# The last batch of a cross-attention and FFN kernel: row sums ahead of the last tile's products, and VectorE normalising straight out of the accumulator

## What is computed

```python
# x (8, 56, 128), ctx (8, 1500, 128), mask (8, 56); all float32
xn = layernorm(x)
q, k, v = heads(xn @ Wq), heads(ctx @ Wk), heads(ctx @ Wv)      # 16 heads of 64
dots = q @ k.T * 64 ** -0.5 - (1 - mask)[:, None, :, None] * 1e6
x = x + merge(softmax(dots) @ v) @ Wout + bout
z = layernorm(x)
x = x + gelu(z @ w1[e] + b1[e]) @ w2[e] + b2[e]                 # e = the batch
```

## Time and profile before

| | |
|---|---|
| three runs | 405.58, 407.91, 409.17 us; median 407.91 us |
| the profiled execution's own time | 405.75 us |
| its span, first to last instruction | 403.9 us |
| PE busy | 390.0 us (97%), 1721 MATMUL records |
| DVE busy | 302.8 us (75%) |
| ACT busy | 206.0 us (51%) |
| mean granted TensorE clock | 1.000 of full speed |
| chain that ended last, by engine | PE 90%, DVE 5%, ACT 2% |

### The profile page before, as it was taken

The page is one execution under the profiler, slowest core; times in us unless marked ns, Lnnn a source line. Parts: engine busy times, 40 slices in busy tenths (PEclk is TensorE's granted clock), DMA queues, the critical chain, the costliest instruction groups (busy, mean ns, idle before and its releaser), DMA issues.

```text
span 403.9 us, 5555 instructions
## 1 busy us (share of the span) xinstructions
PE 390.0 (97%) x1721; PEld 281.2 (70%) x1721; DVE 302.8 (75%) x490; ACT 206.0 (51%) x274; POOL 57.6 (14%) x47
## 2 busy tenths in 40 slices
PE   7998999999999999999999999999999999999995
PEld 6665666767675877767776877667766777676684
DVE  4889678877887689877887689787887686365443
ACT  3546354565457444665455454565357444746431
POOL 0603400600060000600060001500150000000000
PEclk9999999999999999999999999999999999999999
DMA  7660020040005000042004000160011001100000
GB/s 252 210 199 21 2 76 1 12 142 0 2 4 148 2 2 2 25 155 81 0 18 135 0 0 0 43 193 26 0 35 42 0 0 53 57 2 0 3 2 3
DMA packets 20661, 19.62 MB, mean 49 GB/s; under 512 B 904, under 2 KB 17576, under 8 KB 20648
## 3 DMA queue, kind: packets, MB, share of 16 engines
q1 hardware_dynamic: 20648, 19.45, 15.7%
HBM read 19.21 MB, written 0.23 MB: 48 GB/s over the span
## 4 chain that ended last, share of the span: by engine, by line
PE 90%; DVE 5%; ACT 2%; issue 1%; DMA 1%; SPq 0%; ACTq 0%; DVEq 0%
PE ps_a L426 35%; PE ps_s L398 28%; PE ps_x L434 10%; PE ps_x L453 4%; PE ps_x L441 3%; PE ps_a L373 2%; PE ps_x L473 2%; PE ps_x L482 2%; PE ps_s L412 2%; DMA ex<-in_wk_t 1%; DVE log_sum L793 1%; DVE ctxt_hi L782 1%; ACT inv_sum L635 1%; PE ps_s L528 1%; PE ps_x L412 1%
## 5 line engine op out<-in xcount | busy, mean ns | idle before, releaser
L426 PE MATMUL ps_a<-ex,ctx_sb 125*128 125x448 f32 x384 | 172.1, 541 | 0.0
L605 ACT ACTIVATE ex<-ps_s 125x896 f32<-125x896 f32 x96 | 88.0, 917 | 117.4 <-PE ps_s L398 91.3
L765 DVE TENSOR_REDUCE chunk_max<-ps_x 128x1 f32<-128x500 f32 x168 | 111.3, 674 | 32.6 <-PE ps_x L434 29.5
L434 PE MATMUL ps_x<-ctxt_hi,qk_hi 128*128 128x500 f32 x168 | 88.5, 530 | 6.3 <-DVE log_sum L793 3.6
L426 PEld LDWEIGHTS ps_a<-ex,ctx_sb 125*128 125x128 f32 x384 | 71.4, 189 | 27.5 <-issue 21.6
L762 DVE TENSOR_TENSOR ex_sum<-ex_sum,ex 125x896 f32<-125x896 f32 x80 | 86.6, 1083 | 4.6 <-ACT ex L605 4.6
L398 PE MATMUL ps_s<-qk_hi,ctxt_hi 128*125 128x448 f32 x192 | 87.2, 535 | 0.0
L612 ACT COPY ps_s<-shift_row 125x896 f32<-125x896 f32 x80 | 72.9, 911 | 9.9 <-DVE shift_row L882 7.8
L398 PEld LDWEIGHTS ps_s<-qk_hi,ctxt_hi 128*125 128x125 f32 x192 | 35.8, 187 | 35.5 <-issue 35.1
L398 PE MATMUL ps_s<-qk_hi,ctxt_lo 128*125 128x448 f32 x192 | 57.3, 379 | 0.0
L1008 POOL TENSOR_TENSOR qk_lo<-qk,qk_hi 128x448 fp32r<-128x448 f32 x16 | 23.7, 1483 | 218.9 <-DVE qk_hi L786 218.1
(11 more groups left out here) (79 smaller groups left out, 263.3 us busy)
## 6 DMA issues: line engine op xcount, KB each, us to landing
ctxt_raw<-in_ctx_t SPq DMA_DIRECT2D x8, 750.0 KB, 7.4
ctx_sb<-in_ctx SPq DMA_DIRECT2D x8, 750.0 KB
w_sb<-in_w SPq DMA_DIRECT2D x4, 512.0 KB, 3.8
w_sb<-in_w SPq DMA_DIRECT2D x8, 256.0 KB, 4.4
ex<-in_wq_t SPq DMA_DIRECT2D x2, 256.0 KB, 3.9
ex<-in_wk_t SPq DMA_DIRECT2D x2, 256.0 KB, 4.8
att_n<-in_wv_t SPq DMA_DIRECT2D x1, 512.0 KB, 5.9
att_n<-in_w_out SPq DMA_DIRECT2D x1, 512.0 KB, 7.1
```

The lines of the kernel that those rows point to most:

```text
L426: mm = nc.tensor.matmul(ps_a[:, c, 0:CH], ctx_sb[0:MT, u, t, :], ex[0:MT, t % RING, c * CH:(c + 1) * CH], start=(t == 0), stop=(t == TM - 1))
L434: nc.tensor.matmul(bank[:, 0:MC], qk_hi[:, u, t * P:(t + 1) * P], ctxt_hi[:, u, k * MC:(k + 1) * MC], start=True, stop=True).then_inc(job_ ...
L605: nc.scalar.activation(half(ex[0:MT, slot, :]), src, ACT.Exp, scale=SCALE).then_inc(ex_ready, 1)
L765: nc.vector.tensor_reduce(chunk_max[:, k, t:t + 1], filled()[:, 0:MC], AX.X, ALU.max).then_inc(job_free, 1)
```

## The change

Three things, all behind the last batch's tiles. On TensorE the row sums (`sum_jobs`) go from behind the products of tile 11 to between those of tile 10 and tile 11, and `keep_clock(14)` ahead of `y_job` becomes `keep_clock(4)`. On ScalarE the copy `att_out` goes away. On VectorE a new `normalise_last` reads `ps_a` where `normalise_att` read `att`; it waits for the products of tile 11 itself (`pv_done`).

```diff
             iteration(last, prepare=False, pair=Pair(None, ROUNDS, half=0))
-            for t in range(TM - 2, TM):
-                probs_ctx(last, t)
+            probs_ctx(last, TM - 2)
             sum_jobs(last)
+            probs_ctx(last, TM - 1)
             pair = Pair(None, ROUNDS, half=1)
-            keep_clock(14)
+            keep_clock(4)
             y_job(pair)
...
             iteration(last, prepare=False, pair=Pair(None, ROUNDS, half=0))
-            att_out(last)
             inverse_sums(last)
...
+            def normalise_last(b, c):
+
+                dve.wait_ge(pv_done, b.at(TM, TM))
+                nc.vector.tensor_tensor(att_n[:, c * HP:(c + 1) * HP, TOK * b.parity:TOK * b.parity + N],
+                                        ps_a[:, c, 0:CH].rearrange("p (h n) -> p h n", n=N),
+                                        inv_sum[:, c * CH:(c + 1) * CH].rearrange("p (h n) -> p h n", n=N),
+                                        ALU.mult).then_inc(att_n_ready, 1)
...
                 drain_sum(last, c)
                 refine_inverse(c * HP, (c + 1) * HP)
-                normalise_att(last, c * HP, (c + 1) * HP)
+                normalise_last(last, c)
```

## The result

| | before | after |
|---|---|---|
| median of 13 runs | 406.21 us (405.34 to 409.17) | 404.16 us (403.56 to 406.46) |
| ratio | | 0.9946, 95% interval 0.9923 to 0.9968 |
| profiled execution: span | 403.9 us | 403.2 us |

The changed kernel is 0.54% faster; 0.47% (1.91 us) was forecast. The last additions of the two profiles differ by only 0.7 us, because this execution came 1.12 us later to the place where the change begins: the seventh batch's `out_job` starts at 379.06 before and at 380.18 after. Most of that difference is there by 38 us, in a part of the program that the change doesn't touch: the same exp of ScalarE (L605) starts at 37.22 before and at 38.31 after.

A forecast was written before the change was run, and what follows sets the result against it. The end was taken to be set by TensorE's fillers, with sums, logarithm, exp, drain, refine and normalise behind them. Gain 1.56 + 0.37 - 0.02 = 1.91 us gave 403.84 or 406.00, so 405.0 us in the middle, range 403.3 to 407.4.

The forecast's parts named there:

- Fillers on the chain, `y_job` held by 0.37 us: Ahead of y_job on TensorE: it could begin at 388.29 but fillers hold it until 388.66, 0.37 us.
- Sums 1.50 us earlier without a wait: TensorE's row sums, moved ahead of tile 11's four records, start 1.50 us earlier; last add_tile leaves 1.14 us of slack.
- The copy worth 0.06 us: ScalarE ahead of the logarithm: the 0.91 us copy lies beside the sums, so removing it gains only 0.06 us.
- The other half of that step: With sums ahead of tile 11, a copy must wait for tile 11 and would hold up a ready logarithm; edits belong together.
- VectorE out of the accumulator at no price: Normalising from PSUM costs the same as from SBUF, by rows of 620 and 625 ns; dearer normalisation had chance 0.12.
- The additional 65 ns for each: Estimate from the skill page: each of the two PSUM normalisations 65 ns longer, the gain some 0.1 us smaller; not adopted.
- The slack ahead of its wait: VectorE's first normalisation, newly waiting for tile 11's products, may start from 385.64, 0.32 us in time.
- The second half comes just in time: Within y_job: ninth head reached at 388.56, its input usable at 388.58, so a wait of 0.02 us.
- The gap ahead of `y_job`: With eight filler records, TensorE idles about 0.24 us before y_job, waiting for VectorE, in place of none.
- The clock: Granted clock stays 1.00 through y_job; rival: it falls behind eight fillers, 1.7 to 6.7 us slower, chance 0.05.
- My price for a fall through `y_job`: If the granted clock fell to 1.2 GHz in the gap, y_job would take 3.65 us more.
- The sum from the median of three runs: Whole kernel: median of three earlier runs less the 1.91 us gain, 406.00 us; upper of two sums around 405.0.

The follow-up runs named there:

- The copy kept: Kernel before with the sums ahead of tile 11 and 4 fillers, ScalarE's copy staying ahead of the logarithm; median 409.50 us, ratio to before 1.0064.
- the two kernels at 9.24 us: Kernel before with only keep_clock(14) cut to 4, and changed kernel with sums back behind tile 11; last addition ends at 22.71 and 22.70 us.
- the repeat: Changed kernel, unaltered, timed again beside a version with tile 11's halves apart; 12 runs, median 404.20 us, ratio to before 0.9968.
- the 3.3 us gap: TensorE idle ahead of y_job in the kernel before with early sums, 4 fillers and the copy kept; y_job took 5.35 us, ratio to before 1.0064.
- the 3.0 us gap: TensorE idle ahead of the transpose in the changed kernel without its three keep_clock calls; last addition at 22.89 us, ratio to before 1.0006.

## Why the prediction was right, point by point

**Fillers on the chain, `y_job` held by 0.37 us.** Right: 0.36 measured with the fillers alone.

**Sums 1.50 us earlier without a wait.** Right: the sum records start at 3.38 us from the anchor, where they were at 4.88. The moved matmuls are worth exactly their own length, 9.24 to 7.73 between late and early sums.

**The copy worth 0.06 us.** Wrong in size: it is 0. I had taken the 0.04 us from the end of the products to the copy, and put the same between the first sum and a logarithm without the copy. The logarithm starts 1.01 us after the first sum record with the copy (before: 383.94 to 384.95) and without it (after: 383.56 to 384.57). From the end of the second sum record, as the profile counts it, that is 0.09 us and not 0.04 (after: 383.94 + 0.54 = 384.48 to 384.57). In the kernel before, the copy would have let it go at the same moment: where the logarithm waited for the copy alone ("The copy kept"), it started 0.80 us after the copy's start, and 384.14 + 0.80 is 384.94. So it moved by 1.50 us and not by 1.56. The other half of that step, that the copy may not stay once the sums are early, was right and matters more: 10.73 in place of 7.73.

**VectorE out of the accumulator at no price.** Right: 624 ns, against 624 to 626 from SBUF. The additional 65 ns for each that I had worked out from the Trainium skill ("Perfetto Trace Analysis", Optimizing Scalar/DVE Operations) doesn't show, neither here nor between the two kernels at 9.24 us. The slack ahead of its wait was there too, 0.27 us where I had 0.32: with the chain 0.75 us earlier, it becomes an idle of 0.48.

**The second half comes just in time.** Right: `y_job` takes 3.72 us where it took 3.71, so the ninth head waits for next to nothing.

**The gap ahead of `y_job`.** I said 0.24 and it is 0.29: `y_job` came 0.06 later than forecast, as the logarithm did.

**The clock.** Right for this change, granted 1.00 through `y_job`. The step behind it, that a longer gap is needed for a fall, was shown from both sides: no fall behind 1.18, 1.80 and 1.82 us, a fall behind 3.01 and, in eight of nine executions as far as their mean clock tells, behind 3.30. Nothing between 1.82 and 3.01 us was run. My price for a fall through `y_job` was too high, 3.65 us where 1.63 was measured, because the clock fell only within `y_job` and came back within it.

**The absolute time.** 405.0 forecast, 404.16 measured. The sum from the median of three runs (406.00) was high since two of those three were over 407.5; with the median of 13, 406.21 less 1.91 is 404.30. The 405.0 was the middle between two sums and rested on no mechanism. That the medians differ by 2.05 us, so near the forecast, owes something to luck: the tails differ by 1.86, and the repeat gave 1.73. The spread that I could not explain lies in part in the opening, in its waits and its clock.

## What to carry to other kernels

When fillers stand on the chain of waits, the path behind them is the true bound: find the wait that they cover, shorten the path, and cut the fillers with it. Here the shorter path without fewer fillers gave nothing, and fewer fillers without the shorter path gave 0.36 of 1.87 us. An operation on an engine that waits in order costs what it holds up and not its length: the same 0.91 us copy cost nothing beside late sums, and with early sums it delayed `y_job`'s start by 3 us. For gains under 1%, count from an anchor just ahead of the change in the profile, where stretches repeat to 0.02 us while whole executions vary by some 4.

## What the runs showed of the hardware

TensorE's granted clock held at the 2.4 GHz level through idle gaps of up to 1.82 us in the tail. It fell to the 1.2 GHz level behind gaps of 3.0 and 3.3 us, and not at the gap's end but some 0.4 and 0.7 us later (between 390.40 and 390.50 behind a gap that ended at 390.04, and between 395.0 and 395.4 behind one that ended at 394.42). After the 3.3 us gap it came back within the dense `y_job`; after the 3.0 us gap, with sparse products, it stayed at 0.50 to the end. One of nine executions with the 3.3 us gap recorded a mean of 1.000. In the opening of the kernel it fell in one of 13 profiles, where it cost 1.6 us on 16 matmul records. ScalarE's logarithm started 0.09 us after the end of the matmul that released it, its copy 0.04 us after, so such a step is best read for the very instruction that waits. A VectorE operation of 128x448 took 624 ns with one source in the accumulator and 624 to 626 ns with both in SBUF.
